# The second attention rewritten: features as a polynomial in the charge, W_v times W_out formed once, row sums from a column of ones, batches written out three deep

## The chip, the core and the metric

The kernel runs on one core of a Trainium2 chip. Times are microseconds of that core for one launch. PE is the matrix engine (PEld its weight loads), DVE the vector engine, ACT the scalar engine with its function tables, POOL the general-purpose engine, SP the engine that issues most DMAs. They run side by side, each in the order of its own queue, and wait for one another by semaphores.

## What is computed

One layer of four parts over x of 32 batches x 256 rows x 128 columns, each behind a normalisation over the columns: attention a, an expert network, attention b, the same expert network again. The change touches attention b alone, and the loading of its rows. There one batch element of the kernel's 8192 rows is 256 rows long:

```python
q = jnp.tanh(x @ W_charge.T + b_charge)[..., 0]
phi_c = mags * q[..., None] ** jnp.arange(ORDER + 1)
shell = x @ W_shell.T + b_shell
shell = shell / jnp.maximum(jnp.linalg.norm(shell, axis=-1, keepdims=True), 1e-12)
proj = shell @ omega.T + rff_bias
phi_s = jnp.concatenate([jnp.cos(proj), jnp.sin(proj)], axis=-1) * rff_scale
tp = (phi_c[..., :, None] * phi_s[..., None, :]).reshape(b, n, -1)
phi = tp @ W_combine.T
T = jnp.exp(-DIST_COUPLING * jnp.abs(idx[:, None] - idx[None, :]).astype(x.dtype) / DIST_SCALE)
logits = jnp.einsum('bnd,bmd->bnm', phi, phi) * T / temp
logits = jnp.where(causal, logits, -jnp.inf)
attn = jax.nn.softmax(logits, axis=-1)
V = x @ W_v.T + b_v
out = jnp.einsum('bnm,bmd->bnd', attn, V)
return out @ W_out.T + b_out
```

ORDER is 4, so five powers of q (q is the charge, one number per row) times 64 phases (32 cosines, 32 sines) make 320 products per row, which W_combine takes to 64 features.

## The kernel before

`build` runs the parts as phases, one after the other, with a barrier of all engines between them. x stays in SBUF as 64 tiles of 128 rows (`PER` = 2 tiles make a batch element). All arithmetic spoken of here is in fp32 except one small bf16 matmul that adds the causal bar.

`load_rows` brings x back from DRAM in 8 loads of 8 tiles, and DVE takes the statistics of each tile as it lands (L1379). `statistics` makes mean and deviation of them.

`features` (L1396 on) begins with constants: PE multiplies the shell weights by omega (L1469, L1470), DVE scales that into `w_all` and `b_all`, ACT makes the temperature with four small activations and two table loads (L1500 to L1503) and DVE scales `decay` by it (L1546 to L1549). Then 16 rounds of four tiles follow: ACT normalises (L1510), PE turns (L1477), ACT copies, PE multiplies by `w_all`, 225 columns (L1489), DVE adds the bias and keeps 97 columns as `feat` and 128 as `values` (L1556, L1558). At the end come the norm, the reduction of the angle, tanh for the charge, sine and cosine into `phases`, and five `powers` of the charge with their factors (L1583 to L1586).

`attend` (L1589 on) goes over the 32 batch elements, g, in a loop of two per round with the first and the last ones written out; buffers are double, `par` is the parity. Each engine has a queue of its own order:
- POOL: `products(g+2)` forms the 320 products of two tiles (L1685); `values_and_bias(g+1)` copies the values (L1693) and adds b_out to x (L1694).
- PE: `combine(g+1)` multiplies the turned products by W_combine (L1726, three matmuls of 256 columns); `turn_products(g+2)`, six transposes (L1719); `turn_probs(g)`, three (L1744); `scores(g+1)` (L1734 to L1738); `output(g-1)`, times W_out (L1760); `mix(g)`, probabilities times values (L1752, L1753).
- ACT: `exponentials(g)` with their sums (L1805), `copy_phi(g+1)` (L1795), `copy_products(g+2)` (L1788), `copy_o(g)` (L1812).
- DVE: `copy_probs(g)` (L1842), `logits(g+1)` with their maxima (L1832 to L1837), `add(g-1)`: x plus the output over the sum (L1846, L1852), and the statistics of x (L1856).

The order is the one in which the functions are called in each engine's `turn`; nothing else sorts it. The rows name the tiles: `tp` products, `phi_t` features, `prob` probabilities, with `p_` ahead for PSUM; `_at` is `attend`, `_fe` is `features`, `_ab` both.

## Time and profile before

| | us |
|---|---|
| time, median of 3 runs (1427.21 to 1427.66) | 1427.29 |
| span of the profiled execution | 1485.4 |
| PE busy | 1157.9 (78%) |
| DVE busy | 901.1 (61%) |
| POOL busy | 809.1 (54%) |
| ACT busy | 701.1 (47%) |
| `load_rows`, first to last row statistic | 907.06 to 921.8 |
| `features` | 927 to 991 |
| `attend` | 991 to 1138 |

The profile is of one execution, and its span is longer than the times without a profile. Busy shares are means over stages with different limits; a change inside one stage is read from that stage's waits. A row of the timeline gives the start, the duration of the merged instructions, and in brackets how long the engine had been idle and what released it. Every fp32 matmul shows as two passes in the count at a row's end, a transpose as one.

### The profile page before, as it was taken

What the parts mean: (1) busy time and instruction counts of PE and PEld (TensorE: products, weight loads), DVE (VectorE), ACT (ScalarE), POOL (GpSimd) and SP (SyncE); (2) the same over time, 40 slices, a digit from 0 to 9 for tenths busy, and PEclk for the clock granted to TensorE, in tenths of its full rate; (3) what the DMA queues carried; (4) which work ended last, traced back from release to release, by engine and by line L of the source; (5) the groups of instructions that cost most, each with busy time, mean ns of one, the idle gap of its engine ahead of it and who ended that gap; (6) DMA issues with size and microseconds to landing.
All of it is one profiled execution on the core that took longest, in us unless ns stands there. A gap on an engine that the chain in (4) does not pass through costs nothing. (4 is left out here: it accounts for less than half of the span.)

```text
span 1485.4 us, 33918 instructions
## 1 busy us (share of the span) xinstructions
PE 1157.9 (78%) x11356; PEld 745.3 (50%) x11356; DVE 901.1 (61%) x2806; ACT 701.1 (47%) x1485; POOL 809.1 (54%) x712
## 2 busy tenths in 40 slices
PE   0799999999999975468888680849996647888864
PEld 0244444444444433136676460739995315666743
DVE  4377767777777657787775004665556787777300
ACT  0467677676776745512223230945553722223222
POOL 0387878878788760036667751025551003667756
PEclk9999999999999997569999795869998757999977
DMA  6000000000000004403333325000000621333323
GB/s 166 8 2 0 0 0 0 0 0 0 0 0 0 1 2 129 131 20 51 50 52 66 58 25 120 0 0 1 0 0 21 173 71 26 51 66 53 56 46 28
DMA packets 82316, 54.64 MB, mean 37 GB/s; under 512 B 12865, under 2 KB 73665, under 8 KB 82241
## 3 DMA queue, kind: packets, MB, share of 16 engines
q1 hardware_dynamic: 59712, 36.89, 8.9%
q0 software_dynamic: 22528, 16.79, 8.7%
q8 instruction: 42, 0.69, 0.2%
q14 instruction: 34, 0.27, 0.1%
HBM read 28.49 MB, written 25.17 MB: 36 GB/s over the span
## 5 line engine op out<-in xcount | busy, mean ns | idle before, releaser
L352 POOL TENSOR_TENSOR patt_aa<-patt_aa,causal_aa 128x512 f32<-128x512 f32 x256 | 319.3, 1275 | 73.6 <-DVE patt_aa L476 71.8
L476 DVE TENSOR_TENSOR patt_aa<-p_second_aa,first_aa 128x512 f32<-128x512 f32 x384 | 247.3, 686 | 136.3 <-ACT first_aa L409 132.5
L409 ACT ACTIVATE first_aa<-p_first_aa 128x512 f32<-128x512 f32 x384 | 208.5, 596 | 139.0 <-PE p_first_aa L567 135.1
L1330 POOL DMA_INDIRECT rows_e<-norm_rows,index_e x128 | 127.3, 994 | 247.0 <-DVE index_e L1046 209.2
L567 PE MATMUL p_second_aa<-q_t_aa,k_t_aa 32*128 32x512 f32 x768 | 235.7, 642 | 0.0
L567 PE MATMUL p_first_aa<-q_t_aa,k_t_aa 32*128 32x512 f32 x768 | 217.4, 642 | 15.7 <-ACT first_aa L409 15.4
L1178 PE MATMUL p_y_e<-w_e,hid_e 128*128 128x128 f32 x1024 | 148.4, 287 | 12.7 <-issue 12.4
L586 PEld LDWEIGHTS p_z_aa<-patt_aa,v_aa 128*32 128x32 f32 x3072 | 72.4, 109 | 147.5 <-issue 80.4
L1246 PE MATMUL p_cnt_e<-reach_e,ones_e 128*128 128x240 bf16 x448 | 86.8, 324 | 75.8 <-DVE reach_e L1092 73.3
L1178 PEld LDWEIGHTS p_y_e<-w_e,hid_e 128*128 128x128 f32 x1024 | 134.1, 202 | 15.8 <-issue 15.7
L1168 PE MATMUL p_h_e<-rows_t_e,w_e 128*128 128x512 f32 x256 | 139.4, 662 | 0.1
L1339 POOL DMA_INDIRECT ffn_rows<-yb_e,index_e x64 | 101.0, 1578 | 58.6 <-ACT yb_e L1305 38.9
L1339 POOL DMA_INDIRECT out<-yb_e,index_e x64 | 101.8, 1591 | 56.8 <-ACT yb_e L1305 38.4
L1297 ACT ACTIVATE hid_e<-p_h_e,b_e 128x512 f32<-128x512 f32 x128 | 87.9, 687 | 83.4 <-PE p_h_e L1168 80.7
L586 PE MATMUL p_z_aa<-patt_aa,v_aa 128*32 128x128 f32 x3072 | 124.1, 279 | 2.8 <-POOL patt_aa L352 2.8
L1287 ACT ACTIVATE rows_t_e<-p_t_e,bias,gain 128x512 f32<-128x512 f32 x32 | 25.0, 782 | 175.9 <-PE p_t_e L1159 155.7
L567 PEld LDWEIGHTS p_first_aa<-q_t_aa,k_t_aa 32*128 32x128 f32 x768 | 57.7, 183 | 97.9 <-ACT first_aa L409 88.7
L346 POOL TENSOR_TENSOR roped_aa<-straight_aa,crossed_aa 128x512 f32<-128x512 f32 x64 | 81.5, 1273 | 44.7 <-DVE crossed_aa L466 44.7
L1246 PEld LDWEIGHTS p_cnt_e<-reach_e,ones_e 128*128 128x128 bf16 x448 | 38.3, 108 | 122.1 <-DVE reach_e L1092 93.9
L1305 ACT ACTIVATE yb_e<-p_y_e 128x512 f32<-128x512 f32 x32 | 19.1, 598 | 144.7 <-remote 88.4
L1168 PEld LDWEIGHTS p_h_e<-rows_t_e,w_e 128*128 128x128 f32 x256 | 71.1, 316 | 32.4 <-issue 27.4
L396 ACT ACTIVATE q_t_aa<-p_turn_aa,own_aa 128x512 f32<-128x512 f32 x128 | 81.5, 697 | 2.5 <-PE p_turn_aa L550 2.5
(242 smaller groups left out, 2188.7 us busy)
## 6 DMA issues: line engine op xcount, KB each, us to landing
norm_rows<-norm_n SPq DMA_DIRECT2D x32, 256.0 KB, 2.4
w_e<-L_ffn_w SPq DMA_DIRECT2D x32, 256.0 KB
ffn_rows<-x SPq DMA_DIRECT2D x8, 512.0 KB, 3.2
x<-ffn_rows SPq DMA_DIRECT2D x8, 512.0 KB, 7.6
out<-x SPq DMA_DIRECT2D x8, 512.0 KB, 3.2
rows_e<-norm_rows,index_e POOLq DMA_INDIRECT x128
b_e<-L_ffn_b SPq DMA_DIRECT2D x16, 64.0 KB
ffn_rows<-yb_e,index_e POOLq DMA_INDIRECT x64
```

The costliest lines, as they stand in the source:

```text
L346: pool.tensor_tensor(roped[:, t, :, :, :].rearrange("p s h e -> p (s h e)"), straight[:, t, :, :].rearrange("p s e -> p (s e)"), crossed[: ...
L352: pool.tensor_tensor(patt[n % LAG][:, b, :, :], patt[n % LAG][:, b, :, :], causal[:, None, :].broadcast_to([P, 4, P]), ALU.mult).then_inc( ...
L409: act.activation(first[n % 2][:, b, :], p_first[b][:], ACT.Identity).then_inc(first_copied, 1)
L476: dve.tensor_tensor(patt[n % LAG][:, b, :, :].rearrange("p h q -> p (h q)"), p_second[(2 * n + b) % ROOMS][:], first[n % 2][:, b, :], ALU. ...
L567: pe.matmul(out[:], k_t[par][rows, half, keys * P:(keys + 1) * P], q_t[par][rows, half, :, queries * P:(queries + 1) * P], start=True, sto ...
L586: mm = pe.matmul(p_z[32 * c:32 * c + 32, queries * P:(queries + 1) * P], v[par][:, keys, 32 * h:32 * h + 32], patt[n % LAG][:, b, c, :], s ...
L1168: pe.matmul(p_h[m % 2][:], w1[par][:, f:F:FC], rows_t[:, h * 512:(h + 1) * 512], start=True, stop=True).then_inc(up_done, 1)
L1178: mm = pe.matmul(p_y[t // 4][:, (t % 4) * D:(t % 4 + 1) * D], hid[:, f, t * P:(t + 1) * P], w2[par][:, f, :], start=False, stop=(f == FC - 1))
L1246: mm = pe.matmul(p_cnt[:, 0:SPAN * CANDS], ones[:], reach[:, q // 2, :, (q % 2) * SPAN:(q % 2 + 1) * SPAN], start=(q == 0), stop=(q == TIL ...
L1297: act.activation(hid[:, f, h * 512:(h + 1) * 512], p_h[m % 2][:], ACT.Gelu_apprx_tanh, bias=b1[par][:, f:f + 1]).then_inc(gelu_done, 1)
L1330: pool.indirect_dma_start(rows[lpar][:, j, :], None, norm_rows, bass.IndirectOffsetOnAxis(ap=list_of(l, lpar)[:, j:j + 1], axis=0)).then_i ...
L1339: pool.indirect_dma_start(ffn_rows, bass.IndirectOffsetOnAxis(ap=list_of(c, par)[:, j:j + 1], axis=0), yb[par][:, j, :], None, compute_op= ...
```

## The change

In `load_rows`, now `load_rows_and_fold_weights`, ahead of the row statistics on each engine's queue: the constants of `features` move here; W_v and b_v are turned and multiplied by W_out, b_out is added, and the results stand in `w_all` and `b_all` where W_v and b_v were; W_combine is scaled by the factors of the powers into `w_powers` (three blocks of 64 columns; the rows of a block are an even power over an odd one).

In `features` the values come out already multiplied by W_out, in 129 columns of which the last is set to one; `phases` has a second half per tile; instead of the powers the charge, its square and its fourth power are kept.

In `attend` POOL multiplies the 64 phases by the charge into the second half, PE turns these 128 columns (one transpose per tile) and multiplies them by `w_powers` (192 columns per tile); DVE multiplies the second and third block by square and fourth power and adds the first to the second (`combine`); POOL adds the two (`finish_phi`); PE turns phi back. Probabilities times the 129 columns give output and sum at once; DVE inverts the sum (`invert`), ACT scales (`scale_y`), POOL adds to x (`add`). The products with W_out, the copies of values and the bias sum are gone, and so are the sums in the exponentials. All 32 batch elements are written out, and the queues' orders are those of the three-deep loops at the end of the diff.

```diff
-        phase(nc, load_rows, k, ffn_rows)
+        phase(nc, load_rows_and_fold_weights, k, ffn_rows)
...
+            @block.tensor
+            def _(pe):
+                pe.wait_ge(k["b_consts"], 16 * 18)
+                pe.matmul(p_w[:, 0:RFF], k["w_shell"][:], k["omega_t"][:], start=True, stop=True)
+                pe.matmul(p_w[:, RFF:2 * RFF], k["b_shell"][:], k["omega_t"][:], start=True, stop=True)
+                pe.transpose(p_w[:, P:2 * P], k["w_all"][:, VALUE], k["ident"][:])
+                pe.transpose(p_w[:, 2 * P:3 * P], k["b_all"][:, VALUE], k["ident"][:]).then_inc(turned, 1)
+                pe.wait_ge(copied, 2)
+                pe.matmul(p_v[:, 0:D], w_v[:], k["w_out"][:], start=True, stop=True)
+                pe.matmul(p_v[:, D:2 * D], b_v[:], k["w_out"][:], start=True, stop=True).then_inc(folded, 1)
...
+                act.activation(small[0][:], k["temp"][:], ACT.Abs).then_inc(softened, 1)
...
+                act.activation(small[3][:], k["temp"][:], ACT.Relu).then_inc(softened, 1)
...
+                dve.wait_ge(turned, 1)
+                dve.tensor_copy(w_v[:], p_w[:, P:2 * P]).then_inc(copied, 1)
+                dve.tensor_copy(b_v[:], p_w[:, 2 * P:3 * P]).then_inc(copied, 1)
+                dve.tensor_scalar(k["w_all"][:, SHELL + 1:FEAT], p_w[:, 0:RFF], 1.0 / (2 * math.pi), None, ALU.mult).then_inc(step, 1)
+                dve.tensor_scalar(k["b_all"][:, SHELL + 1:FEAT], p_w[:, RFF:2 * RFF], 1.0 / (2 * math.pi), None, ALU.mult).then_inc(step, 1)
+                dve.tensor_scalar(k["b_rff"][:], k["b_rff"][:], 1.0 / (2 * math.pi), None, ALU.mult).then_inc(step, 1)
+                for m in range(NM + 1):
+                    part = slice(64 * (m % 2), 64 * (m % 2) + 64)
+                    of = min(m, ORDER)
+                    dve.tensor_scalar(k["w_powers"][part, m // 2, :], k["w_comb"][part, m // 2, 0:2 * RFF],
...
+                dve.tensor_scalar(k["decay"][:], k["decay"][:], small[5][:, 0:1], None, ALU.mult).then_inc(step, 1)
+                dve.wait_ge(folded, 1)
+                dve.tensor_copy(k["w_all"][:, VALUE], p_v[:, 0:D]).then_inc(step, 1)
+                dve.tensor_tensor(k["b_all"][:, VALUE], p_v[:, D:2 * D], k["b_out"][:], ALU.add).then_inc(step, 1)
+                for g in range(steps):
+                    dve.wait_ge(loaded[g], 16)
+                    for n in range(g * per, (g + 1) * per):
+                        dve.bn_stats(k["halves"][:, n, :], k["x"][:, n, :]).then_inc(measured, 1)
...
+        values = keep("values", [P, TILES, D + 1])
+        phases = keep("phases", [P, TILES, 2, 2, RFF])
+        charge = keep("charge", [P, TILES])
+        square = keep("square", [P, TILES, 2])
...
-                link(act.activation(small[0][:], temp[:], ACT.Abs))
-                link(act.activation(small[1][:], small[0][:], ACT.Exp, scale=-1.0))
-                link(act.activation(small[2][:], small[1][:], ACT.Ln, bias=1.0))
-                link(act.activation(small[3][:], temp[:], ACT.Relu))
...
+                link(dve.memset(values[:, :, D:D + 1], 1.0))
...
+                link(dve.tensor_tensor(square[:, :, 0], charge[:], charge[:], ALU.mult))
+                link(dve.tensor_tensor(square[:, :, 1], square[:, :, 0], square[:, :, 0], ALU.mult))
...
+                def products(b):
+                    tiles = slice(PER * b, PER * b + PER)
+                    pool.tensor_tensor(phases[:, tiles, 1, :, :].rearrange("p t a f -> p t (a f)"),
+                                       phases[:, tiles, 0, :, :].rearrange("p t a f -> p t (a f)"),
+                                       charge[:, tiles, None].broadcast_to([P, PER, W]), ALU.mult).then_inc(tp_done, 1)
+
+                def finish_phi(b):
+                    pool.wait_ge(sums_done, b + 1)
+                    if b >= 2:
+                        pool.wait_ge(phi_turned, b - 1)
+                    pool.tensor_tensor(phi[b % 2][:, :, 0:W], sums[b % 2][:, :, 0, :], sums[b % 2][:, :, 1, :], ALU.add).then_inc(phi_done, 1)
+
+                def add(b):
+                    tiles = slice(PER * b, PER * b + PER)
+                    pool.wait_ge(y_scaled, PER * b + PER)
+                    pool.tensor_tensor(k["x"][:, tiles, :], k["x"][:, tiles, :], y[b % 2][:], ALU.add).then_inc(x_done, 1)
+
+                for i in range(2):
+                    pool.memset(phi[i][:, :, W:P], 0.0).then_inc(padded, 1)
+                for b in range(4):
+                    products(b)
+                for i in range(-3, B):
+                    if i >= 0 and there(i + 4):
+                        products(i + 4)
+                    if there(i):
+                        add(i)
+                    if there(i + 3):
+                        finish_phi(i + 3)
 
             @block.tensor
...
+                def terms(b):
+                    pe.wait_ge(tp_copied, b + 1)
+                    if b >= 2:
+                        pe.wait_ge(sums_done, b - 1)
+                    for t in range(PER):
+                        mm = pe.matmul(p_terms[b % 2][:, t * TRIPLE:(t + 1) * TRIPLE], tp_t[b % 2][:, t * P:(t + 1) * P],
+                                       w_powers[:].rearrange("p m e -> p (m e)"), start=True, stop=True)
...
+                def turn_phi(b):
+                    if b < 2:
+                        pe.wait_ge(padded, 2)
+                    pe.wait_ge(phi_done, b + 1)
+                    if b >= 2:
+                        pe.wait_ge(phi_copied, b - 1)
+                    for t in range(PER):
+                        at = (b % 2) * T + t * P
+                        mm = pe.transpose(p_phi[:, at:at + P], phi[b % 2][:, t, :], k["ident"][:])
+                    mm.then_inc(phi_turned, 1)
...
+                def mix(b):
+                    pe.wait_ge(pt_copied, b + 1)
+                    if b >= 1:
+                        pe.wait_ge(y_scaled, PER * b)
+                    pt = prob_t[b % 2]
+                    pe.matmul(p_y[:, 0:D + 1], pt[:, 0:P], values[:, PER * b, :], start=True, stop=True)
+                    pe.matmul(p_y[:, T:T + D + 1], pt[:, P:T], values[:, PER * b, :], start=True, stop=False)
+                    pe.matmul(p_y[:, T:T + D + 1], pt[:, T:384], values[:, PER * b + 1, :], start=False, stop=True).then_inc(y_done, 1)
+
+                for i in range(-3, B):
+                    if there(i):
+                        turn_probs(i)
+                    if there(i + 3):
+                        turn_products(i + 3)
+                    if there(i + 2):
+                        turn_phi(i + 2)
+                    if there(i):
+                        mix(i)
+                    if there(i + 3):
+                        terms(i + 3)
+                    if there(i + 2):
+                        scores(i + 2)
...
+                def scale_y(b):
+                    act.wait_ge(r_done, b + 1)
+                    if b >= 2:
+                        act.wait_ge(x_done, b - 1)
+                    for t in range(PER):
+                        act.activation(y[b % 2][:, t, :], p_y[:, t * T:t * T + D], ACT.Identity, scale=rmass[b % 2][:, t:t + 1]).then_inc(y_scaled, 1)
+
+                for i in range(-3, B):
+                    if there(i):
+                        copy_probs(i)
+                    if there(i + 3):
+                        copy_products(i + 3)
+                    if there(i + 2):
+                        copy_phi(i + 2)
+                    if there(i + 1):
+                        exponentials(i + 1)
+                    if there(i):
+                        scale_y(i)
...
+                def combine(b):
+                    dve.wait_ge(terms_done, b + 1)
+                    if b >= 2:
+                        dve.wait_ge(phi_done, b - 1)
+                    tiles = slice(PER * b, PER * b + PER)
+                    src = p_terms[b % 2][:, 0:PER * TRIPLE].rearrange("p (t m e) -> p t m e", t=PER, m=3)
+                    dve.tensor_tensor(sums[b % 2][:], src[:, :, 1:3, :], square[:, tiles, :, None].broadcast_to([P, PER, 2, W]),
+                                      ALU.mult).then_inc(scaled, 1)
+                    dve.wait_ge(scaled, b + 1)
+                    dve.tensor_tensor(sums[b % 2][:, :, 0, :], sums[b % 2][:, :, 0, :], src[:, :, 0, :], ALU.add).then_inc(sums_done, 1)
...
+                def invert(b):
+                    dve.wait_ge(y_done, b + 1)
+                    if b >= 2:
+                        dve.wait_ge(y_scaled, PER * (b - 1))
+                    dve.reciprocal(rmass[b % 2][:], p_y[:, :].rearrange("p (t e) -> p t e", t=PER)[:, :, D]).then_inc(r_done, 1)
...
+                for i in range(-3, B + 2):
+                    if there(i + 1):
+                        logits(i + 1)
+                    if there(i - 2):
+                        measure(i - 2)
+                    if there(i):
+                        invert(i)
+                    if there(i + 3):
+                        combine(i + 3)
```

PE in the middle of `attend`, one batch element, before (`w_comb` is W_combine):

```order
L1726 MATMUL p_phi_at<-tp_t_at,kept_w_comb 128x256 x3
L1719 MATMUL p_tp_at<-ident,tp_at 128x128 x6
L1744 MATMUL p_pt_at<-ident,prob_at 128x128 x3
L1734 MATMUL p_s_at<-phi_t_at 128x128
L1735 MATMUL p_s_at<-kept_bar,kept_ident_b 128x128
L1736 MATMUL p_s_at<-phi_t_at 128x128
L1737 MATMUL p_s_at<-phi_t_at 128x128
L1738 MATMUL p_s_at<-kept_bar,kept_ident_b 128x128
L1760 MATMUL p_y_at<-kept_w_out,o_t_at 128x128 x2
L1752 MATMUL p_o_at<-prob_t_at,v_at 128x256
L1753 MATMUL p_o_at<-prob_t_at,v_at 128x128
```

And the same place after:

```order
L1761 MATMUL p_pt_at<-ident,prob_at 128x128 x3
L1722 MATMUL p_tp_at<-ident,phases_ab 128x128 x2
L1742 MATMUL p_phi_at<-ident,phi_at 128x128 x2
L1769 MATMUL p_y_at<-values_ab,prob_t_at 128x129
L1770 MATMUL p_y_at<-values_ab,prob_t_at 128x129
L1771 MATMUL p_y_at<-values_ab,prob_t_at 128x129
L1730 MATMUL p_terms_at<-kept_w_powers,tp_t_at 128x192 x2
L1750 MATMUL p_s_at<-phi_t_at 128x128
L1751 MATMUL p_s_at<-kept_bar,kept_ident_b 128x128
L1752 MATMUL p_s_at<-phi_t_at 128x128
L1753 MATMUL p_s_at<-phi_t_at 128x128
L1754 MATMUL p_s_at<-kept_bar,kept_ident_b 128x128
```

The combining matmuls and the output product left; the transposes of phi came in ahead of the mix, the terms behind it.

ACT in the middle of `attend`, two batch elements in a row, after (`y` is the scaled output, `p_pt` the turned probabilities):

```order
L1813 ACTIVATE prob_t_at<-p_pt_at 128x384
L1793 ACTIVATE tp_t_at<-p_tp_at 128x256
L1799 ACTIVATE phi_t_at<-p_phi_at 128x256
L1807 ACTIVATE prob_at<-logit_at,ntop_at 128x128
L1807 ACTIVATE prob_at<-logit_at,ntop_at 128x256
L1820 ACTIVATE y_at<-p_y_at,rmass_at 128x128 x2
L1813 ACTIVATE prob_t_at<-p_pt_at 128x384
L1793 ACTIVATE tp_t_at<-p_tp_at 128x256
```

The copy of the turned probabilities came from DVE, the scaling of y is new behind the exponentials, and the copy of `p_o` is gone.

POOL at the same place after:

```order
L1687 TENSOR_TENSOR phases_ab<-phases_ab,charge_ab 128x2x64
L1700 TENSOR_TENSOR x<-x,y_at 128x256
L1695 TENSOR_TENSOR phi_at<-sums_at 128x2x64
L1687 TENSOR_TENSOR phases_ab<-phases_ab,charge_ab 128x2x64
L1700 TENSOR_TENSOR x<-x,y_at 128x256
L1695 TENSOR_TENSOR phi_at<-sums_at 128x2x64
```

The sum with y stands between the products and the last sum of phi.

## Rows read from the trace of the kernel before

**Rows 1.** Busy time by engine in `attend`: stretch, length, busy (instructions), clock, DMA.

```profile
core 0: us, PE busy (x) PEld busy (x) DVE busy (x) ACT busy (x) POOL busy (x), PEclk, DMA share, GB/s
991.00:1138.00 147.00, 141.30 (x992) 129.95 (x992) 80.44 (x352) 79.45 (x258) 78.64 (x130) 0.97 0.00 0
```

**Rows 2.** Who waited for whom, 1005 to 1125 us, the longest two.

```profile
engine line waited for: us in total, times, longest us
POOL v_at L1693 <- PE p_o_at L1753: 50.9, 28, 1.8
ACT o_t_at L1812 <- PE p_o_at L1753: 48.9, 28, 1.7
```

**Rows 3.** Timeline of PE, one batch of `attend`: start, duration, instruction, shapes, passes.

```profile
1042.37 0.38 PE L1753 MATMUL p_o_at<-prob_t_at,v_at 128*128 128x128 f32 x2
1042.59 1.46 PE L1726 MATMUL p_phi_at<-tp_t_at,kept_w_comb 128*128 128x256 f32 x6
1043.88 0.82 PE L1719 MATMUL p_tp_at<-ident,tp_at 128*128 128x128 f32 x6
1044.54 0.49 PE L1744 MATMUL p_pt_at<-ident,prob_at 128*128 128x128 f32 x3
1044.87 0.39 PE L1734 MATMUL p_s_at<-phi_t_at 128*128 128x128 f32 x2
...
1045.70 0.66 PE L1760 MATMUL p_y_at<-kept_w_out,o_t_at 128*128 128x128 f32 x4
...
1046.86 0.38 PE L1726 MATMUL p_phi_at<-tp_t_at,kept_w_comb 128*128 128x256 f32 x1
```

**Rows 4.** Timeline of ACT in the same batch.

```profile
1042.79 0.38 ACT L1812 ACTIVATE o_t_at<-p_o_at 128x256 f32<-128x256 f32 x1 [1.75 <-PE p_o_at L1753]
1043.07 0.39 ACT L1805 ACTIVATE prob_at<-logit_at,ntop_at 128x128 f32<-128x128 f32 x1
...
1043.45 0.50 ACT L1805 ACTIVATE prob_at<-logit_at,ntop_at 128x256 f32<-128x256 f32 x1
```

**Rows 5.** Timeline of POOL in `attend`.

```profile
1060.36 0.73 POOL L1694 TENSOR_TENSOR x<-x,kept_b_out 128x256 f32 x1
1061.05 1.41 POOL L1685 TENSOR_TENSOR tp_at<-phases_ab,powers_ab 128x320 f32 x2
```

**Rows 6.** Timeline, the first product, the first transposes and the last statistics of `attend`.

```profile
991.94 2.75 POOL L1685 TENSOR_TENSOR tp_at<-phases_ab,powers_ab 128x320 f32<-128x320 f32 x4
...
992.75 1.54 PE L1719 MATMUL p_tp_at<-ident,tp_at 128*128 128x128 f32 x6 [19.98 <-POOL tp_at L1685]
...
1137.38 0.48 DVE L1856 BATCH_NORM_STATS2 halves<-x 128x6 f32<-128x128 f32 x2
```

**Rows 7.** Groups by line and shape: count, busy us, mean ns, idle before.

```profile
L352 POOL TENSOR_TENSOR patt_aa<-patt_aa,causal_aa 128x512 f32<-128x512 f32 x256 | 319.3, 1275 | 73.6 <-DVE patt_aa L476 71.8
...
L389 ACT ACTIVATE v_aa<-p_misc_aa 128x128 f32<-128x128 f32 x64 | 14.5, 291 | 5.8 <-PE p_misc_aa L539 5.8
...
L1558 DVE TENSOR_TENSOR values_ab<-p_f_fe,kept_b_all 128x256 f32 x28 | 11.6, 414 | 0.0
```

**Rows 8.** Timeline, row statistics in `load_rows`, then the head of `features` on ACT.

```profile
907.06 1.65 DVE L1379 BATCH_NORM_STATS2 halves<-x 128x6 f32<-128x128 f32 x8 [89.35 <-DMA x<-ffn_rows]
...
916.81 5.00 DVE L1379 BATCH_NORM_STATS2 halves<-x 128x6 f32<-128x128 f32 x24 [0.85 <-DMA x<-ffn_rows]
...
927.59 0.20 ACT L1500 ACTIVATE small_fe<-kept_temp 128x1 f32<-128x1 f32 x1 [1.76 <-PEq L80]
...
931.09 3.19 ACT L1510 ACTIVATE a_fe<-x,shift,rstd 128x128 f32<-128x128 f32 x8
```

**Rows 9.** Ten microseconds of the second expert stage, columns as in rows 1.

```profile
1290.00:1300.00 10.00, 6.86 (x77) 5.47 (x76) 7.82 (x30) 1.37 (x2) 6.56 (x5) 1.00 0.26 29
```

**Rows 10.** First expert stage: PE after "issue" (timeline), then two stretches.

```profile
707.93 1.04 PE L1178 MATMUL p_y_e<-w_e,hid_e 128*128 128x128 f32 x7 [0.45 <-issue]
...
738.65 0.93 PE L1178 MATMUL p_y_e<-w_e,hid_e 128*128 128x128 f32 x6 [0.44 <-issue]
...
837.12 1.08 PE L1159 MATMUL p_t_e<-ident,rows_e 128*128 128x128 f32 x3 [1.04 <-issue]
...
708.00:738.60 30.60, 27.43 (x211) 20.84 (x211) 22.87 (x89) 8.16 (x12) 21.00 (x16) 0.94 0.33 55
828.50:843.00 14.50, 6.90 (x23) 4.73 (x23) 0.00 (x0) 0.60 (x1) 10.44 (x10) 0.62 0.23 42
```

More of the change, by code:

```diff
@@ L1655, in there @@
[L1655 to L1671 removed]
+        def there(b):
+            return 0 <= b < B
@@ L1755, in output @@
-                def output(g, par):
-                    pe.wait_ge(o_copied, ROOM + g + 1)
-                    pe.wait_ge(x_done, 2 * PER + 2 * g)
-                    for t in range(PER):
-                        mm = pe.matmul(p_y[:, t * D:(t + 1) * D], o_t[par][:, t * P:(t + 1) * P], w_out[:], start=True, stop=True)
-                    mm.then_inc(y_done, 1)
-                turn_products(0, 0)
-                combine(0, 0)
-                turn_products(1, 1)
-                scores(0, 0)
@@ L1803, in exponentials, with copy_phi @@
+                def copy_phi(b):
+                    act.wait_ge(phi_turned, b + 1)
+                    if b >= 2:
+                        act.wait_ge(s_done, b - 1)
+                    act.activation(phi_t[b % 2][:], p_phi[:, (b % 2) * T:(b % 2) * T + T], ACT.Identity).then_inc(phi_copied, 1)
+                def exponentials(b):
+                    act.wait_ge(n_done, b + 1)
+                    if b >= 2:
+                        act.wait_ge(pt_done, b - 1)
                     for t in range(PER):
@@ L1814, in _ @@
-                copy_products(0, 0)
-                copy_phi(0, 0)
-                copy_products(1, 1)
-                def turn(g, par):
-                    exponentials(g, par)
-                    if there(g + 1):
-                        copy_phi(g + 1, 1 - par)
-                    if there(g + 2):
-                        copy_products(g + 2, par)
-                    copy_o(g, par)
-                plan(act, turn)
+                        act.activation(prob[b % 2][:, cols], logit[b % 2][:, cols], ACT.Exp, bias=ntop[b % 2][:, t:t + 1]).then_inc(e_done, 1)
```

325 lines of the change are left out of this document (112 added, 213 removed).

## The prediction

> **What bounds the kernel now.** I read the stretches first, then who waits inside the one that the change rewrites, then one batch of it in order of time. The second attention's loop (`attend`) runs from 991 to 1138 us; in it the matmul engine is busy 141.3 of 147 us at nearly the full granted clock [rows 1]. From 1005 to 1125 us the list of waits holds POOL, ACT and DVE waiting for PE, and no line in which PE waits [rows 2]. One batch is the distance from one `p_phi` to the next, 1042.59 to 1046.86: 4.27 us [rows 3]. So PE's queue is the bound here, and 31 periods of 4.27 are 132.4 of the 145.9 us between the first product, 991.94, and the last statistics, 1137.86 [rows 6]; 13.5 us are filling and draining. The profiled execution's span is 1485.4 us against a median of 1427.29 for the timed runs; 58 us lie between them and the trace doesn't say where. `attend` moves no data by DMA and is paced by engines, so I take its microseconds over as they are; scaled by 1427.29/1485.4 = 0.96 the gain below would be about 1 us smaller. About 0.2%, 2.9 us, is what a measurement can tell from no change.
>
> **PE's work per batch.** Out of [rows 3], by start to start: combine 1.29, six transposes of products 0.66, three of probabilities 0.33, scores 0.83, output and mix together 1.16. The change leaves the probabilities and the scores. It turns two tiles of products instead of six (0.22), turns phi (two more, 0.22), and forms the terms by two matmuls with 192 moving columns. A matmul with 256 columns takes 1.29/3 = 0.43, so 192 take 0.32 and two 0.65. The output product is gone, and mix becomes three matmuls with 129 columns; one with 128 takes 0.22 (1042.37 to 1042.59), so 0.66. Sum: 0.33+0.22+0.22+0.66+0.65+0.83 = 2.91 us, 1.36 less than now. If PE stayed the bound, that would be 42 us. It doesn't stay the bound.
>
> **The other engines' work per batch.** ACT: three plain copies, the exponentials without read-out, and two scaled evictions, about 2.3 us of queue. DVE: logits 0.8, statistics 0.5, a reciprocal 0.17, and combine, two PSUM operations of which the larger has the shape that took 0.414 [rows 7], together 0.7: 2.2 us. POOL: 0.46+0.73+0.46 = 1.65 us (working below). None reaches 2.91. So the time per batch is set by a closed chain of waits.
>
> **The chain that I expect.** In the new order POOL does `add(i)` ahead of `finish_phi(i+3)`, and PE needs that phi for `turn_phi(i+3)`, ahead of `mix(i+1)`. Behind `turn_phi(i+2)` ACT does `copy_phi(i+2)`, `exponentials(i+1)`, `scale_y(i)`, in this order; that eviction releases `add(i)`. From one `turn_phi` round to the next:
> - two transposes, the last lasting 0.27: 0.38 [rows 3]; PE's end to ACT's start 0.04 (1042.75 to 1042.79) [rows 3, 4];
> - `copy_phi`: the same 128x256 eviction is 0.38 long and the next instruction starts after 0.28 [rows 4];
> - exponentials: 0.39 and 0.50 long, each with the same overlap of 0.10, since no read-out of the sums stands behind them any more: 0.69 [rows 4];
> - `scale_y`: a 128x128 eviction takes 0.291 without a pointer operand [rows 7]; the exponential of that size, with one, 0.39 [rows 4]. Two: 0.29+0.39 = 0.68;
> - ACT to POOL: not shown; I take 0.09, as from POOL to PE (991.94+0.72 to 992.75) [rows 5, 6];
> - `add`, 128x256: the next starts after 0.69 [rows 5];
> - `finish_phi`, 128 elements: 512 took 1.275 [rows 7] and 256 took 0.73 [rows 5], so 2.1 ns each, 0.73-0.27 = 0.46; then POOL to PE 0.09.
>
> Sum: 0.38+0.04+0.28+0.69+0.68+0.09+0.69+0.46+0.09 = 3.40 us per batch. `products(i+4)`, 0.46, stands ahead of `add(i)` but waits for nothing, so it lies in the time in which POOL waits for ACT; it costs 0.46 if that cover goes. `combine(i+3)` reaches `finish_phi` earlier than `add(i)` does, by about 0.4 us. `mix(i)`, reciprocal and `scale_y(i)` leave only about 0.1 us; close.
>
> **Sum for attend.** One batch alone through the new queues: POOL's clearing and product 0.9, turn and copy 0.9, terms and combine 1.7, finish 0.55, phi turned and copied 0.9, scores and logits 1.85, exponentials 0.85, probabilities turned and copied 1.1, mix 0.95, reciprocal 0.25, scaling 0.75, add 0.8, statistics 0.55: 12.0 us. PE starts at the lower clock, as it does now: six transposes take 1.54 there [rows 6] and 0.82 later [rows 3]. For the first batch's PE steps I add 2.3. So 14.3 + 31 x 3.40 = 119.7 instead of 145.9: 26.2 us less.
>
> **Written out instead of a loop.** PE's 32 batches of 25 matmul passes now stand once each in the program, 800 passes with a weight load each. In the expert stage, also written out, PE pauses 0.45 us for "issue" at 707.93 and again at 738.65, with 211 passes between [rows 10]. So `attend` would have about four such pauses, 1.8 us, or twice that if every second one lies unseen in another wait; I take 1.8, and 0 to 3.6 for the range. The Trainium skill (Runtime: NRT & Kernel Launch, Instruction fetch mechanics) says that fetch in sequence is hidden behind dispatch and that a taken branch is what stalls it; by that this term is zero and the sum 1.8 us lower. The row shows a pause in straight-line code, so here the row decides.
>
> **The folded weights.** Four small ACTs and two table loads leave the head of `features`: the first normalisation starts at 931.09 behind a chain that began at 927.59 [rows 8], so it moves up by 3.5 us, and PE and DVE of that stage follow it; the clock's rise there moves along. The work goes ahead of the row statistics, where DVE idles until the first load lands at 907.06. Beginning about 903 with PE and ACT, DVE's 17 small operations would end near 908.2, 1.1 us late; but DVE idled 0.85 before 916.81, waiting for a load [rows 8], and a little at each load before that, so it catches up: cost 0, at most 1 us; 5 us if the loads were not there to hide it. The powers' six DVE operations become two squares, both behind ACT's last sine: 0. POOL's copies of values and the bias sum ran in its idle time: 0.
>
> Forecast: 1427.3 - 26.2 - 3.5 + 1.8 = **1399.4, say 1400 us**.
>
> **Rivals.**
> *PE's own queue.* If the POOL tail is shorter than I priced it, the next chain is `turn_probs`, `copy_probs`, `mix`, `terms`, `scores`: 0.33+0.16+0.04+0.49+0.04+0.66+0.65+0.83 = 3.20. Then 14.3+99.2 = 113.5, and 1427.3-32.4-3.5 = 1391.4. For it: it is only 0.2 away. Against: POOL's prices are measured ones.
> *The tail is longer.* `finish_phi` at the price of 256 elements, 0.73, since its blocks of 64 are strided, and scaling like the normalisation with two pointer operands, 8 in 3.19 [rows 8], +0.2: 3.87. Then 14.3+120 = 134.3, and 1427.3-11.6-3.5 = 1412.
> *Instructions come late.* From 828.5 to 843 us PE issues only 23 matmul passes, with up to 1.04 of waiting for nothing shown [rows 10]; at the 0.11 that a pass of 128 columns takes in [rows 3] they need 2.5 us, so such an episode costs 12 us. Two in `attend` would give 1424. Against: that stage has gathers and scatters on the DMA engines, `attend` has none.
> *Slower: the clock falls.* PE would idle 0.5 us in every 3.4, which it doesn't now. At the lower level (1.2 GHz) PE's 2.91 become 5.82, PE is the bound again, and `attend` takes 9+32x5.82 = 195 us: 1427.3+49.3-3.5 = 1473. A batch at that level costs 2.4 more than one at 2.4 GHz, so from 12 of 32 batches on the gain is lost. Against: in ten microseconds of the expert stage PE was busy for only 6.86, and the granted clock was 1.00 [rows 9]. The Trainium skill (TensorE: Matmul & The Clock Gate, A second HAM failure mode) describes a matmul loop whose short idle times between groups were enough to make the clock go back and forth; the trace of this kernel disagrees so far. And at the lower level PE has no idle time left, which would raise the clock again.
>
> **How the numbers follow.** POOL chain (1400) 0.54, PE queue (1391) 0.15, longer tail (1412) 0.17, late instructions (1424) 0.06, lower clock (1473) 0.08. The first three hold 0.86; their bounds are 1389, with the issue term at zero, and 1413. Faster 0.86 plus half of the late-instruction case, 0.89; same 0.03; slower 0.08.
>
> **What the new profile would show.** Period of `p_phi` transposes 3.4 us; PE idle about 0.5 per batch, put down to POOL ahead of `p_phi`; POOL's `add` waiting for ACT's `y`; granted clock 1.00 in the loop; ACT's first normalisation right behind the barrier, no table load ahead of it; the row statistics ending as late after the first DMA as before. I am wrong if PE waits for DVE's combine or for `prob_t` instead, if POOL's 128-element sum isn't near 0.46, or if the clock in the loop is below 1.00.

## The result and the profile after

The changed kernel takes 1396.08 us (median of 4 runs, 1395.69 to 1396.29); beside it the kernel before took 1427.42. The ratio is 0.9781, with a 95% interval from 0.9767 to 0.9795. The forecast was 1400, from 1389 to 1413. The time is in the range; the chain that I named turned out to be one of two closed chains of the same length.

The timeline of the changed kernel gives the ends of the stages, in the columns of [rows 6] and [rows 8]:

```profile
871.87 12.08 SPq L1392 DMA_DIRECT2D x<-ffn_rows  x8
...
885.95 4.94 DVE L1442 BATCH_NORM_STATS2 halves<-x 128x6 f32<-128x128 f32 x24 [0.18 <-DMA x<-ffn_rows]
891.72 0.06 DVE L212 MEMSET eps_b<- 128x1 f32 x1 [0.83 <-PEq L80]
...
957.38 1.47 POOL L1687 TENSOR_TENSOR phases_ab<-phases_ab,charge_ab 128x128 f32<-128x128 f32 x4
...
1074.45 0.48 DVE L1867 BATCH_NORM_STATS2 halves<-x 128x6 f32<-128x128 f32 x2 [1.11 <-POOL x L1700]
1076.27 0.06 DVE L212 MEMSET eps_n<- 128x1 f32 x1 [1.33 <-PEq L80]
```

In the trace of before the loads are issued at 902.98, the first instruction of the statistics (`eps_b`) stands at 922.61, and `eps_n` at 1138.86; the others are in [rows 6, 8]. So the stretches compare:

| stretch | before | after | moved | forecast |
|---|---|---|---|---|
| loads issued to last row statistics | 18.83 | 19.02 | +0.2 | 0, at most +1 |
| `eps_b` to first product (`features`) | 69.33 | 65.66 | -3.7 | -3.5 |
| first product to last statistics (`attend`) | 145.92 | 117.55 | -28.4 | -26.2 |
| PE waiting for its instructions in `attend` | 0 | 0 | 0 | +1.8 |
| last statistics to `eps_n` | 1.00 | 1.34 | +0.3 | 0 |

They add up to -31.5 us before rounding; the medians differ by 31.3.

One period in the middle of `attend`, after, lines of PE and its weight loads, ACT, POOL and DVE in order of time; in brackets the idle time of the engine before the group and what ended it:

```profile
1019.66 0.49 ACT L1813 ACTIVATE prob_t_at<-p_pt_at 128x384 f32<-128x384 f32 x1 [0.99 <-PE p_pt_at L1761]
...
1019.95 0.20 PEld L1742 LDWEIGHTS p_phi_at<-ident,phi_at 128*128 128x128 f32 x2 [0.34 <-POOL phi_at L1695]
1019.95 0.44 PE L1742 MATMUL p_phi_at<-ident,phi_at 128*128 128x128 f32 x2
...
1020.21 0.30 PEld L1769 LDWEIGHTS p_y_at<-values_ab,prob_t_at 128*128 128x128 f32 x2
1020.22 0.48 PE L1769 MATMUL p_y_at<-values_ab,prob_t_at 128*128 128x129 f32 x2
1020.42 0.38 ACT L1799 ACTIVATE phi_t_at<-p_phi_at 128x256 f32<-128x256 f32 x1
...
1020.53 0.39 PE L1770 MATMUL p_y_at<-values_ab,prob_t_at 128*128 128x129 f32 x2
...
1020.70 0.79 ACT L1807 ACTIVATE prob_at<-logit_at,ntop_at 128x128 f32<-128x128 f32 x2
...
1020.98 0.81 PE L1730 MATMUL p_terms_at<-kept_w_powers,tp_t_at 128*128 128x192 f32 x4
1021.18 0.17 DVE L1862 RECIPROCAL rmass_at<-p_y_at 128x2 f32<-128x2 f32 x1 [0.52 <-PE p_y_at L1771]
1021.39 0.62 ACT L1820 ACTIVATE y_at<-p_y_at,rmass_at 128x128 f32<-128x128 f32 x2
...
1021.63 0.38 PE L1750 MATMUL p_s_at<-phi_t_at 128*128 128x128 f32 x2
...
1022.09 0.72 POOL L1700 TENSOR_TENSOR x<-x,y_at 128x256 f32<-128x256 f32 x1 [1.84 <-ACT y_at L1820]
...
1022.47 0.49 PE L1761 MATMUL p_pt_at<-ident,prob_at 128*128 128x128 f32 x3
...
1022.77 0.46 POOL L1695 TENSOR_TENSOR phi_at<-sums_at 128x128 f32<-128x128 f32 x1
...
1023.28 0.44 PE L1742 MATMUL p_phi_at<-ident,phi_at 128*128 128x128 f32 x2
```

The period is 1023.28 - 1019.95 = 3.33 us (it was 4.27 [rows 3]), and the chain of the forecast can be walked: `p_phi` 1019.95, `phi_t` 1020.42, exponentials 1020.70, `y` 1021.39, `add` 1022.09, `finish_phi` 1022.77, `p_phi` 1023.28. I call it the POOL tail. Nothing waits longer than a handover on it, which looks like the proof. But a second chain, PE's loop, can be walked just as tightly: probabilities turned 1022.47 less 3.33 = 1019.14, `prob_t` 1019.66 (its bracket says that ACT waited for it), mix 1020.22, terms 1020.98, scores 1021.63, probabilities 1022.47. This too is 3.33 us (0.52 + 0.56 + 0.76 + 0.65 + 0.84), and PE's idle time lies within its first two links, while PE has no `prob_t` yet. The trace can't say which of the two sets the pace, or whether both do. That is what the experiments are for.

The two also cross: from `p_phi` over mix (1020.22) and the reciprocal (1021.18) one comes to `y` at the same 1021.39, since the reciprocal ends at 1021.35 and the exponentials hand over at 1020.70 + 0.69 = 1021.39. This path shares the POOL tail from `y` on, so whatever takes `add` out of the tail takes it away as well.

The clock was 1.00 in the middle of `attend`; busy time by engine there, columns as in [rows 1]:

```profile
985.00:1055.00 70.00, 67.69 (x527) 61.13 (x526) 45.94 (x210) 49.29 (x148) 31.42 (x63) 1.00 0.01 1
```

### The profile page after: what moved, and what is told of

The parts are those of the page before. It is cut to its first block and busy times, and to the rows that moved or that the text cites. A ratio compares the mean times of both kernels' runs of the same rounds, so it can differ in the third digit from the quotient of the medians.

```text
span 1393.9 us, 32681 instructions
## 1 busy us (share of the span) xinstructions
PE 1097.0 (79%) x11170; PEld 698.2 (50%) x11170; DVE 889.4 (64%) x2781; ACT 697.6 (50%) x1452; POOL 779.8 (56%) x680
## 5 line engine op out<-in xcount | busy, mean ns | idle before, releaser
L1179 PE MATMUL p_y_e<-w_e,hid_e 128*128 128x128 f32 x1024 | 135.3, 275 | 0.0
L1247 PE MATMUL p_cnt_e<-reach_e,ones_e 128*128 128x240 bf16 x448 | 83.8, 318 | 63.5 <-DVE reach_e L1093 63.5
L1179 PEld LDWEIGHTS p_y_e<-w_e,hid_e 128*128 128x128 f32 x1024 | 124.6, 192 | 0.0
L568 PEld LDWEIGHTS p_second_aa<-q_t_aa,k_t_aa 32*128 32x128 f32 x768 | 76.3, 183 | 0.0
```

Of the source, the lines that this page charges most:

```text
L568: pe.matmul(out[:], k_t[par][rows, half, keys * P:(keys + 1) * P], q_t[par][rows, half, :, queries * P:(queries + 1) * P], start=True, sto ...
L1179: mm = pe.matmul(p_y[t // 4][:, (t % 4) * D:(t % 4 + 1) * D], hid[:, f, t * P:(t + 1) * P], w2[par][:, f, :], start=False, stop=(f == FC - 1))
L1247: mm = pe.matmul(p_cnt[:, 0:SPAN * CANDS], ones[:], reach[:, q // 2, :, (q % 2) * SPAN:(q % 2 + 1) * SPAN], start=(q == 0), stop=(q == TIL ...
```

## The experiments

The first expert stage, whose code is the same in all these kernels, doesn't end at the same moment in each: the loads behind it are issued between 869.65 and 872.77 us. So a difference of 2 us between two medians may come from there, and each experiment is also read by its own stretch of the trace: period, the length of `attend` (first product to last statistics, 117.55 in the changed kernel), or `features`. Each kernel is the changed kernel with the edit named; its median comes from 4 runs where nothing else is said.

**POOL's order alone.**

```diff
-                    if there(i):
-                        add(i)
                     if there(i + 3):
                         finish_phi(i + 3)
+                    if there(i):
+                        add(i)
```

> The changed kernel with one edit: POOL does finish_phi(i+3) ahead of add(i), so add and the eviction in front of it no longer stand between combine and phi. Theory A, the prediction's: the POOL tail alone sets the 3.33 us per batch that the new trace shows, and PE's own queue would do 3.20. Then 31 x 0.13 = 4 us are gained: 1392. Theory B: PE's queue (turn_probs, copy_probs, mix, terms, scores) takes 3.33 as well, since copy_probs starts 0.53 behind turn_probs, mix 0.05 behind copy_probs, and mix 0.78, terms 0.65 and scores 0.83 follow without a gap in the trace: 0.53+0.49+0.05+0.78+0.65+0.83 = 3.33. Then the time stays at 1396 (within 0.7), and only the idle time ahead of p_phi goes elsewhere in the batch.

Measured: 1395.03 us (ratio to before 0.9775, 0.9758 to 0.9791), period 3.333, `attend` 117.56. Nothing is gained, although `add` and the evictions no longer stand ahead of `finish_phi`. Who waited for whom, 985 to 1055 us, of the changed kernel (columns as in [rows 2]):

```profile
POOL x L1700 <- ACT y_at L1820: 38.6, 21, 1.9
...
PEld p_phi_at L1742 <- POOL phi_at L1695: 7.3, 21, 0.4
```

and of this one:

```profile
POOL phi_at L1695 <- DVE sums_at L1845: 38.5, 21, 1.8
...
PEld p_phi_at L1742 <- POOL phi_at L1695: 4.8, 21, 0.2
PEld p_y_at L1769 <- ACT prob_t_at L1813: 3.6, 21, 0.2
```

POOL now waits for DVE's sums and no more for `y`. Of PE's wait a part has moved: 0.2 us stays ahead of `p_phi`, and 0.2 appears ahead of `p_y`, where PE waits for `prob_t`. Theory A, by which the POOL tail alone sets the pace, falls.

**PE's queue alone: mix one batch later.** Mix, reciprocal, scaling, add and statistics move one round back in the four engines' queues, and mix stands ahead of `turn_phi`; the loops run one round further.

```diff
                     if there(i + 3):
                         turn_products(i + 3)
+                    if there(i - 1):
+                        mix(i - 1)
                     if there(i + 2):
                         turn_phi(i + 2)
-                    if there(i):
-                        mix(i)
...
-                    if there(i):
-                        scale_y(i)
+                    if there(i - 1):
+                        scale_y(i - 1)
...
-                    if there(i - 2):
-                        measure(i - 2)
-                    if there(i):
-                        invert(i)
+                    if there(i - 3):
+                        measure(i - 3)
+                    if there(i - 1):
+                        invert(i - 1)
...
-                    if there(i):
-                        add(i)
+                    if there(i - 1):
+                        add(i - 1)
```

> The changed kernel with the other edit: mix, and with it reciprocal, scaling, add and statistics, one batch later in every queue, and mix ahead of turn_phi, so that PE's queue no longer stands still for copy_probs; POOL's order is left as it was. Theory A (POOL tail alone): 3.33 per batch stays, and one round more to drain costs 0 to 2: 1396 to 1398. Theory B (two loops of equal length): the same, 1396 to 1398. A third theory C, that PE's queue alone is the bound and POOL's wait in the trace is only its shadow: PE's 2.92 per batch, 31 x 0.41 = 12.7 less a drain of 2: 1385.

Measured: 1396.32 us (0.9785, 0.9769 to 0.9802), period 3.332, `attend` 118.87: the same pace and 1.3 us more to drain. PE waits for POOL still, and no more for `prob_t`, which was ready long before; the first line is from the waits from 985 to 1055 us, the others from the timeline:

```profile
PEld p_phi_at L1742 <- POOL phi_at L1695: 6.1, 21, 0.3
...
1020.32 0.44 PE L1742 MATMUL p_phi_at<-ident,phi_at 128*128 128x128 f32 x2
...
1022.61 0.30 PEld L1769 LDWEIGHTS p_y_at<-values_ab,prob_t_at 128*128 128x128 f32 x2
...
1022.71 0.39 PE L1769 MATMUL p_y_at<-values_ab,prob_t_at 128*128 128x129 f32 x2
...
1022.94 0.39 PE L1770 MATMUL p_y_at<-values_ab,prob_t_at 128*128 128x129 f32 x2
...
1023.65 0.44 PE L1742 MATMUL p_phi_at<-ident,phi_at 128*128 128x128 f32 x2
```

So PE's queue isn't the bound alone either; theory C falls. The reciprocal (1020.25) ends well before the scaling (1021.76) here, and the pace is the same, so the POOL tail through the exponentials needs no help from the crossing path.

**Both edits.**

> Both edits together. Theory B: neither loop is left, and PE's work of 2.92 us per batch is the bound: 31 x 0.41 = 12.7 us less, the longer drain gives 1 to 2 back: 1385. Theory A expects what its first edit alone gives, 1392, and a little more from PE's queue: 1388 to 1392. Theory C expects 1385 here too, but has it already without the POOL edit.

Measured: 1385.82 us (0.9715, 0.9699 to 0.9731), period 3.014, `attend` 109.55. Two edits that give nothing apart give 8.0 us of `attend` together (the other 2 between the medians lie outside it: the loads are issued at 870.64 instead of 871.87, and the rest is in the stages behind). PE is the bound now. Its busy time from 985 to 1055 us, first with POOL's order alone changed, then with both edits:

```profile
985.00:1055.00 70.00, 70.00 (x527) 61.12 (x526) 50.35 (x210) 49.32 (x148) 31.50 (x63) 1.00 0.01 1
...
985.00:1055.00 70.00, 70.00 (x584) 67.08 (x583) 51.60 (x233) 54.77 (x164) 34.30 (x69) 1.00 0.01 2
```

The busy share can't tell the two apart, for it hides waits of 0.2 us. What tells them apart is that the 584 matmul passes are 57 more than the 527 of the changed kernel in the same 70 us, and that no line in the list of waits has PE or its weight loads waiting. The period is 0.1 above my 2.92. Part of that can be seen: scores start 0.08 after `phi_t` lands (1020.26 + 0.38 to 1020.72) and take 0.91 from there to the turning of the probabilities (1021.63) instead of 0.84. This kernel beats both others.

**The same two transposes in two places.** Two more transposes per batch, 0.22 us of PE, written into an unused quarter of a `p_terms` buffer; in the first kernel between `turn_products` and `turn_phi`, in the second between `mix` and `terms`.

```diff
+                def extra(b):
+                    for _ in range(2):
+                        pe.transpose(p_terms[(b + 1) % 2][:, 384:512], k["ident"][:], k["ident"][:])
...
```

> The changed kernel with two more transposes of 128 columns per batch (0.22 us of PE, into an unused part of a PSUM buffer, read by nobody), put between turn_products and turn_phi. Two loops side by side: this place lies in the time in which PE waits for copy_probs and for POOL anyway (0.34 idle ahead of turn_phi): 3.33 per batch, attend 117.6, whole 1396. If PE's summed work is the bound: 3.55 per batch, 31 x 0.22 = 7 more, 1403.

> The same two transposes, put between mix and terms. Two loops side by side: now they lie on PE's loop (turn_probs, copy_probs, mix, terms, scores) and every batch takes 0.22 longer: 3.55, attend 117.6 + 6.9 = 124.5, whole 1403. If only the POOL tail bound, as the prediction had it, they would cost nothing, since the tail does not pass through this place: 3.33 and 1396.

Measured: in the gap 1394.40 us (0.9766, 0.9749 to 0.9782), period 3.333, `attend` 117.59: free. Behind mix 1401.41 us (0.9812, 0.9795 to 0.9828), period 3.554, `attend` 124.15: the full 0.22 per batch. PE's timeline of the second, one period:

```profile
1020.63 0.38 PE L1758 MATMUL p_terms_at<-ident 128*128 128x128 f32 x2
1020.85 0.82 PE L1730 MATMUL p_terms_at<-kept_w_powers,tp_t_at 128*128 128x192 f32 x4
...
1024.18 0.38 PE L1758 MATMUL p_terms_at<-ident 128*128 128x128 f32 x2
```

The distance is 1024.18 - 1020.63 = 3.55. PE's loop is shown by this without a change in POOL's or ACT's order: what lies on it costs its length, and what lies in the gap ahead of `mix` costs nothing.

**Sums from the accumulator again, in both POOL orders.** The sums come from the exponentials' read-outs as before the change, and mix has 128 columns.

```diff
-                        act.activation(prob[b % 2][:, cols], logit[b % 2][:, cols], ACT.Exp, bias=ntop[b % 2][:, t:t + 1]).then_inc(e_done, 1)
+                        act.activation(prob[b % 2][:, cols], logit[b % 2][:, cols], ACT.Exp, bias=ntop[b % 2][:, t:t + 1],
+                                       accum_out=mass[b % 2][:, t:t + 1]).then_inc(e_done, 1)
...
-                    dve.wait_ge(y_done, b + 1)
+                    dve.wait_ge(e_done, PER * b + PER)
...
-                    dve.reciprocal(rmass[b % 2][:], p_y[:, :].rearrange("p (t e) -> p t e", t=PER)[:, :, D]).then_inc(r_done, 1)
+                    dve.reciprocal(rmass[b % 2][:], mass[b % 2][:]).then_inc(r_done, 1)
```

> The changed kernel with one part undone: the sums of the probabilities come from the exponentials' accumulator again (a read-out of 0.19 behind each, as in the rows of before), the reciprocal takes them from there, and mix has 128 columns instead of 129. Both theories: two instructions more on ACT between copy_phi and scale_y; in before the pair with its read-outs takes about 0.90 from start to start, now 0.69. The POOL tail gets 0.2 longer, 3.53 per batch, 31 x 0.2 = 6: 1402. If the read-outs hid in ACT's idle time the time would stay at 1396.

> The changed kernel with the sums from the accumulator again and, besides, finish_phi ahead of add on POOL. If the POOL tail and PE's queue are two loops that bind side by side, the read-outs now lie on neither: 3.33 us per batch again instead of the 3.51 of the accumulator alone, attend 117.6 us, the whole 1396. If the accumulator costs ACT or PE time in itself, 3.51 stays, attend 122.8.

Measured: with the change's POOL order 1398.40 us (0.9805, 0.9789 to 0.9821), period 3.513, `attend` 122.75; with `finish_phi` first 1395.16 us (0.977, 0.9754 to 0.9786), period 3.334, `attend` 117.55. ACT in the first of the two:

```profile
1021.32 0.39 ACT L1809 ACTIVATE prob_at<-logit_at,ntop_at 128x128 f32<-128x128 f32 x1
...
1021.62 0.19 ACT L1809 ACTIVATION_READ_ACCUMULATOR prob_at<-logit_at,ntop_at 128x1 f32 x1
1021.71 0.49 ACT L1809 ACTIVATE prob_at<-logit_at,ntop_at 128x256 f32<-128x256 f32 x1
...
1022.11 0.19 ACT L1809 ACTIVATION_READ_ACCUMULATOR prob_at<-logit_at,ntop_at 128x1 f32 x1
1022.20 0.61 ACT L1824 ACTIVATE y_at<-p_y_at,rmass_at 128x128 f32<-128x128 f32 x2
```

From the first exponential to the scaling it is 0.88 us, against 0.69 with the ones column: 0.19 more, and the period is longer by 0.18. So the POOL tail is a loop that binds too, and the ones column is worth 5.2 us of `attend`, but only in this order: where `finish_phi` stands first, the read-outs cost nothing. The median of the first was 3.6 us below what I expected; 2.1 of them lie ahead of the loads (issued at 869.74).

**The new formulas two batches deep.** Every function of `attend` as in the changed kernel; only the queues differ, and POOL does `finish_phi` ahead of `add`. PE's:

```diff
-                for i in range(-3, B):
-                    if there(i):
-                        turn_probs(i)
-                    if there(i + 3):
-                        turn_products(i + 3)
-                    if there(i + 2):
-                        turn_phi(i + 2)
-                    if there(i):
-                        mix(i)
-                    if there(i + 3):
-                        terms(i + 3)
-                    if there(i + 2):
-                        scores(i + 2)
+                for i in range(-2, B):
+                    if there(i + 2):
+                        turn_products(i + 2)
+                    if there(i + 1):
+                        turn_phi(i + 1)
+                    if there(i):
+                        turn_probs(i)
+                    if there(i + 2):
+                        terms(i + 2)
+                    if there(i + 1):
+                        scores(i + 1)
+                    if there(i):
+                        mix(i)
```

> The new formulas (polynomial behind W_combine, W_v times W_out formed first, ones column) with every function of attend unchanged, but the queues written two batches deep instead of three: products of batch i+2, phi, scores and exponentials of i+1, probabilities and mix of i in one round, finish_phi ahead of add. Theory of the loops: one batch's chain turn_products, copy, terms, combine, finish_phi must now pass within one round, and with it phi, scores, logits and exponentials within the next; I work it out to 4.3 us per batch although PE still has only 2.9 us of work: attend 145, whole 1423 to 1425. Rival: the smaller work on PE is the gain itself, and the depth adds little: 3.4 to 3.6 per batch, attend 121 to 126, whole 1400 to 1404.

Measured: 1426.08 us (10 runs), ratio to before 0.9994 (0.9984 to 1.0003); period 4.308, `attend` 148.41. In this order the smaller work on PE gives nothing: `attend` is 2.5 us longer than before, and only the gain in `features` keeps the total level. Who waited for whom from 985 to 1060 us, ACT's longest and PE's two, and then the busy time:

```profile
ACT prob_at L1807 <- DVE ntop_at L1856: 35.2, 17, 2.1
...
PE p_pt_at L1761 <- ACT prob_at L1807: 10.4, 17, 0.6
...
PE p_terms_at L1730 <- ACT tp_t_at L1793: 4.3, 18, 0.2
```

```profile
985.00:1060.00 75.00, 60.31 (x437) 51.68 (x436) 34.08 (x171) 39.06 (x123) 27.20 (x53) 1.00 0.00 1
```

PE is busy for 60.3 of 75 us and waits inside each round for scores, logits, exponentials and the turning of the probabilities to pass one after the other. This is one two-deep order, the best that I could work out from the rows; others weren't tried.

**The temperature's chain back in `features`.** The four ACT operations and the four of DVE leave the load stage for the head of `features`.

```diff
                 link = Chain(act, ast)
+                soften = Chain(act, softened)
+                soften(act.activation(small[0][:], k["temp"][:], ACT.Abs))
+                soften(act.activation(small[1][:], small[0][:], ACT.Exp, scale=-1.0))
+                soften(act.activation(small[2][:], small[1][:], ACT.Ln, bias=1.0))
+                soften(act.activation(small[3][:], k["temp"][:], ACT.Relu))
...
```

> The changed kernel with one part undone: the four small ACT operations with their two table loads, and the four DVE operations on the temperature, stand at the head of features again. Prediction's theory: they delay the first normalisation by 3.5 us and all of features with it: from the statistics' first instruction to the first product of attend 68.8 us instead of 65.3; whole 1399.6. Rival: the time is taken up later in features, where DVE waits for ACT's sines anyway: 65.3 and 1396.

Measured: 1399.45 us (0.9801, 0.9784 to 0.9817); from `eps_b` to the first product 69.79 instead of 65.66, 4.1 more; `attend` 117.40. The head of ACT's queue, in that kernel:

```profile
895.78 0.20 ACT L1529 ACTIVATE small_fe<-kept_temp 128x1 f32<-128x1 f32 x1 [1.76 <-PEq L80]
...
899.28 3.19 ACT L1539 ACTIVATE a_fe<-x,shift,rstd 128x128 f32<-128x128 f32 x8
```

The chain is 3.50 long here as well. In the changed kernel the first normalisation stands at 896.83 with `eps_b` at 891.72, 5.11 behind; here 8.48 behind, 3.4 later. The other 0.8 come later in `features`; I didn't follow them.

**The fold behind the statistics.** DVE measures the rows first and does its part of the fold afterwards.

```diff
+                for g in range(steps):
+                    dve.wait_ge(loaded[g], 16)
+                    for n in range(g * per, (g + 1) * per):
+                        dve.bn_stats(k["halves"][:, n, :], k["x"][:, n, :]).then_inc(measured, 1)
                 dve.wait_ge(turned, 1)
...
```

> The changed kernel with one move: DVE does the row statistics first and its part of the folded weights behind them. Prediction's theory: ahead of the statistics the fold lies in DVE's wait for the rows, so that it costs 0.2; behind them nothing covers it, and DVE's chain of 3.7 us (873.60 to 877.30 in the new trace) stands in the open: from the issue of the loads to the statistics of b some 3 to 3.7 us more, whole 1399 to 1400. Rival: PE and ACT have done their parts by then, only DVE's own 16 operations remain, about 3 us with no waits among them: 1399. If the loads were not the cover: no change.

Measured: 1397.03 us (0.9788, 0.9772 to 0.9805; 1396.71 to 1398.67). The loads are issued at 871.79 and `eps_b` stands at 894.96: 23.17 us, against 19.85 in the changed kernel, so 3.3 more where I expected 3 to 3.7. The medians differ by 0.95 only, less than the stretch does; the runs of this kernel spread over 2 us, and the profiled one, 3.0 us longer in span than the changed kernel's (1396.9 against 1393.9), is the one that the stretch is read from. So the cover is shown in the trace, and hardly in the medians.

## Why the prediction was right, and where it wasn't

**PE's work per batch, 2.91: right within 0.1.** With both loops out of the way the pace is 3.01, with no wait of PE listed; scores are 0.08 of the difference (0.91 against 0.83).

**The chain through POOL, 3.40: right within 0.06 in every link, 3.33 in sum.** Measured against forecast: `turn_phi` with the handover 0.47 (0.42), `copy_phi` 0.28 (0.28), exponentials 0.69 (0.69), scaling 0.62 (0.68), handover 0.08 (0.09), `add` 0.68 (0.69), `finish_phi` 0.46 (0.46), handover 0.05 (0.09). Over 31 periods the 0.07 are 2.2 us, the whole of what `attend` did better than forecast; 14.3 us for filling and draining was right (117.55 - 31 x 3.333 = 14.2). Two margins beside the chain were smaller than forecast: the reciprocal leaves none (0.1), and `combine` is done 0.2 ahead of `add` (1022.58 against 1022.81) and not 0.4. Neither changed the time.

**That this chain alone sets the pace: wrong.** The step that failed is the price of the rival "PE's own queue", which I set at 3.20 and let count only if the POOL tail were shorter, with a chance of 0.15. From [rows 3] I priced mix at 0.66, three matmuls of 0.22 each. In the new queue its first matmul waits for `prob_t`, which is its weights: the load begins only when ACT is done (1020.21, with the matmul right behind it at 1020.22), and the next matmul starts after 0.31 instead of 0.22 (1020.22 to 1020.53). In the second experiment, where `prob_t` is ready long before, the load begins 0.10 ahead of the matmul and the next one starts after 0.23 (1022.71 to 1022.94). With that mix takes 0.76, and the handover around `prob_t` 0.03 more than I had: the rival is 3.33. Both loops bind side by side. The time came out right because the POOL tail was priced well and the other loop, 0.13 longer than I had it, is no longer than the tail; that last part is luck. The advice that one would have drawn from the prediction, reorder POOL and gain 4 us, would have been wrong, as the first experiment shows.

**What I said the profile would show.** The wait of PE for POOL ahead of `p_phi` is there (0.34 instead of about 0.5), and so is POOL's wait for `y`. Both appeared as forecast, and they prove less than I meant them to. My sign of being wrong, PE waiting for `prob_t`, is in no line of the waits from 985 to 1055 us, although that loop was just as long: a wait names what came last, and the second loop shows only as the 0.07 between the end of `prob_t` (1020.15) and mix (1020.22).

**Written out, +1.8: wrong, it is 0.** Among the changed kernel's waits from 956 to 1076 us no line has PE waiting for "issue" (its weight loads have one, 1.4 us in the first batch, while PE itself waited for POOL). Instructions were fetched meanwhile; the queue of instructions q8 from 956 to 1075 us, with packets, MB and share:

```profile
q8 instruction: 7, 0.11, 0.4%
```

I took the pauses in [rows 10] for a cost of code that is written out. They belonged to that one execution: between 560 and 900 us neither the changed kernel's trace nor that of any experiment has a line in which PE waits for "issue" in the same expert code (its weight loads have some everywhere), where before has

```profile
PE p_y_e L1178 <- issue: 5.9, 12, 0.9
```

(columns as in [rows 2]), and it reaches the loads at 871.87 instead of 902.98 us, 31 earlier. Behind `attend` it is 29 more (346.5 us from `eps_n` to the end of the span before, 317.6 after). Together 60: the profiled execution of before was 58 us above its median, that of after 2 below. What made the instructions late in that execution stays open, and so does whether they account for all of it. The sentence of the Trainium skill (Runtime: NRT & Kernel Launch, Instruction fetch mechanics), by which fetch in sequence is hidden, agrees with `attend` here, and the row of before that I set against it was no evidence on this kernel's `attend`. The rivals at 1391 and 1412 were summed without the 1.8, the forecast with it; as the term measured 0, nothing hangs on that.

**The temperature's chain, -3.5: right** (-3.7; put back, +4.1). **The fold at no cost: right** (+0.2; without its cover +3.3). **The clock: right.** It was 1.00 in each of the three stretches shown, even with PE idle for 14.7 of 75 us.

**The rivals.** Longer tail and late instructions did not occur. The equal length of two loops was not among the cases: I had them as either one or the other.

## What to carry to other kernels

A pipelined loop over several queues has a pace for each closed chain of waits, and the slowest counts; where two are equal, an edit that shortens one gives nothing, and only both together pay. So list all the chains with their lengths before choosing an edit, and test with a small added operation in two places: it costs its full length on a tight chain and nothing in a gap. Taking work from the engine that is the bound can gain nothing by itself if the order then makes this engine wait: here the new formulas in one two-deep order ran level with the old kernel, three deep they gained 28 us of `attend` although PE still waited 0.34 per batch, and with both loops out of the way 36.

## What the runs showed of the hardware

A matmul whose weights are the operand that has just become ready cost 0.09 us more than one in a row of others (0.31 instead of 0.22, the first of three with 129 columns): its weight load began 0.01 ahead of it, where with the weights ready earlier it began 0.10 ahead and the matmul took 0.23. PE's granted clock stayed at 1.00 although PE was idle for some 0.85 us in each 4.31 of the two-deep kernel (14.7 of 75). One profiled execution can be 58 us longer than the timed runs of the same kernel, in the two expert stages; a pause seen there once is no price for another stage. PE's busy share read 70.00 of 70 us in a kernel whose weight loads waited 0.2 us twice per batch; the count of passes in the same stretch (527 against 584) told the difference.
